# A graph layer's loop on one core: the transposed tile moves to another PSUM bank and TensorE's step is put in another order

## The reference

```
h     = relu(layernorm(x))
p1    = tanh(h @ pp_W1 + pp_b1) @ pp_W2 + pp_b2
inter = concat(p1[src], p1[dst]) @ pi_W1 + pi_b1     # per edge
inter = (inter @ pi_W2 + pi_b2) @ pi_W3              # 64 x 8 values
i1    = einsum('ecb,eb->ec', inter.reshape(E, 64, 8), edge_attr_8)
i1    = tanh(i1 @ ii_W1 + ii_b1) @ ii_W2 + ii_b2
out   = x + segment_sum(i1, dst, 6250)
```

## Time and profile before

| | |
|---|---|
| median of the runs | 2601.27 us |
| the profiled execution | 2618.32 us |
| its span | 2616.5 us |
| PE, DVE, ACT, POOL busy | 71%, 53%, 41%, 58% |
| mean granted clock of PE | 0.81 |

### The profile page before, as it was taken

The page is one execution under the profiler, slowest core; times in us unless marked ns, Lnnn a source line. Parts: engine busy times, 40 slices in busy tenths (PEclk is TensorE's granted clock), DMA queues, the critical chain, the costliest instruction groups (busy, mean ns, idle before and its releaser), DMA issues.

```text
span 2616.5 us, 52109 instructions
## 1 busy us (share of the span) xinstructions
PE 1864.1 (71%) x18378; PEld 1177.1 (45%) x18378; DVE 1383.5 (53%) x2286; ACT 1070.9 (41%) x2409; POOL 1521.1 (58%) x1581
## 2 busy tenths in 40 slices
PE   4277777677777767767677767777777767777777
PEld 3144444444444444444444444444444444444445
DVE  5354555555555545545555555455455554555555
ACT  4144444344444444444444444444444433444444
POOL 2666566566566665565666566666556655566660
PEclk8578878888778788788887887887777877887878
DMA  3322222222222222222222122222222122222221
GB/s 104 68 49 46 47 49 43 47 49 45 48 43 48 48 46 48 46 44 48 48 45 49 43 48 48 46 48 49 44 46 50 43 48 41 48 45 43 45 44 38
DMA packets 311278, 125.86 MB, mean 48 GB/s; under 512 B 233399, under 2 KB 283433, under 8 KB 311161
## 3 DMA queue, kind: packets, MB, share of 16 engines
q1 hardware_dynamic: 259985, 73.19, 14.1%
q0 software_dynamic: 50048, 51.35, 10.4%
q10 hardware_dynamic: 1128, 0.26, 0.1%
HBM read 118.67 MB, written 6.00 MB: 48 GB/s over the span
## 4 chain that ended last, share of the span: by engine, by line
PE 59%; issue 16%; another core or an unknown queue 14%; ACT 7%; DVE 2%; SPq 1%; ACTq 0%; DVEq 0%; DMA 0%
PE bank L1041 34%; PE bank L1048 6%; PE bank L1085 6%; PE spread_ps L1033 4%; PE bank L1025 4%; ACT st_sb L538 4%; PE bank L1017 3%; ACT tt_sb L526 2%; DVE o_sb L697 1%; SPq L277 0%; ACT t_sb L529 0%; PE spread_ps L1125 0%; PE bank L921 0%; DMA v_tab<-acc_all 0%
## 5 line engine op out<-in xcount | busy, mean ns | idle before, releaser
L392 POOL DMA_INDIRECT u_rows<-u_tab,src_e x1564 | 1514.7, 968 | 1034.8 <-PE bank L1025 476.8
L1041 PE MATMUL bank<-o_sb,g_sb 128*64 128x256 f32 x6256 | 1025.7, 484 | 284.8 <-issue 232.2
L697 DVE TENSOR_TENSOR o_sb<-st_sb,spread_ps 128x2048 f32<-128x2048 f32 x391 | 891.3, 2280 | 234.5 <-PE spread_ps L1033 134.0
L1041 PEld LDWEIGHTS bank<-o_sb,g_sb 128*64 128x64 f32 x6256 | 569.8, 171 | 580.0 <-issue 458.5
L538 ACT ACTIVATE st_sb<-bank,s_bias 64x256 f32<-64x256 f32 x1564 | 734.1, 469 | 117.6 <-PE bank L1025 83.2
L795 DVE TENSOR_TENSOR acc_all<-acc_all,bank 65x42 f32 x391 | 76.1, 195 | 919.0 <-remote 640.3
L526 ACT ACTIVATE tt_sb<-bank,z_bias 128x256 f32<-128x256 f32 x391 | 185.5, 474 | 753.0 <-PE bank L1041 386.6
L1048 PE MATMUL bank<-ident,tt_sb 128*128 128x128 f32 x782 | 188.2, 326 | 366.7 <-ACT tt_sb L526 234.4
L529 ACT COPY t_sb<-bank 128x256 f32<-128x256 f32 x391 | 146.5, 375 | 618.8 <-remote 340.8
L1085 PEld LDWEIGHTS bank<-hot,t_sb 128*65 128x65 f32 x3128 | 247.5, 156 | 210.4 <-issue 209.5
L1085 PE MATMUL bank<-hot,t_sb 128*65 128x42 f32 x3128 | 298.0, 251 | 10.8 <-issue 10.2
(11 more groups left out here) (109 smaller groups left out, 227.7 us busy)
## 6 DMA issues: line engine op xcount, KB each, us to landing
loc_bc<-loc_tab SPq DMA_DIRECT2D x391, 126.0 KB
u_rows<-u_tab,src_e POOLq DMA_INDIRECT x1564
v_win<-v_tab SPq DMA_DIRECT2D x391, 15.8 KB
basis<-edge_attr SPq DMA_DIRECT2D x24, 256.0 KB
v_tab<-acc_all SPq DMA_DIRECT2D x6, 375.0 KB
u_tab<-basis SPq DMA_DIRECT2D x6, 250.0 KB
out<-x_sb SPq DMA_DIRECT2D x2, 750.0 KB
x_sb<-x SPq DMA_DIRECT2D x3, 375.0 KB
```

The lines of the kernel that those rows point to most:

```text
L392: pool.indirect_dma_start(out=u_rows[:, g % UR, j, :], out_offset=None, in_=u_tab[:, :], in_offset=bass.IndirectOffsetOnAxis(ap=src_e[:, g ...
L697: return nc.vector.tensor_tensor(o_sb[:, r, :, :].rearrange("p c (j e) -> p j c e", j=TILES), st_sb[:, r, :].rearrange("p (j e) -> p j e", ...
L1041: last = nc.tensor.matmul(z_ps[h * D:(h + 1) * D, 0:2 * P], g_sb[:, c, :], o_sb[:, r, c, 2 * h * P:(2 * h + 2) * P], start=(c == 0), stop= ...
```

## The change

t gets two buffers, the free halves of the banks in which s lies (4 and 5), and leaves z's bank. PE's step n is now: s of n, t of n-3, segment sums of n-4, spread of n-1, z of n-2. ACT's step n is: the copy of s of n, the copy of t of n-3, the tanh of n-2. DVE adds the sums of n-5.

With the buffers the waits change. z waits for the tanh of the group before, no longer for the copy of its t. s of n waits for the copy of t of n-4, which leaves the bank that s is written to. t of n-3 waits for the copy of s of n-1, which reads the same bank, and for the copy of t of n-5.

```
-        z_ps, t_ps = bank[6][:, 0:2 * P], bank[6][:, 2 * P:2 * P + TILES * D]
+        z_ps = bank[6][:, 0:2 * P]
+        t_ps = [bank[4][:, 2 * P:4 * P], bank[5][:, 2 * P:4 * P]]
...
+                    if has(n - 3):
+                        g = n - 3
+                        act.wait_ge(t_ps_ready, g + 1)
+                        if g >= 2:
+                            act.wait_ge(seg_ready, g - 1)
+                        copy_t(g % 2).then_inc(t_ready, 1)
                     if has(n - 2):
...
                         tanh_z(g % 2).then_inc(tt_ready, 1)
-                        act.wait_ge(t_ps_ready, g + 1)
-                        if g >= 2:
-                            act.wait_ge(seg_ready, g - 1)
-                        copy_t(g % 2).then_inc(t_ready, 1)
...
-                    if has(n - 4):
-                        g = n - 4
+                    if has(n - 5):
+                        g = n - 5
...
                 if of(0):
                     if of(2):
                         pe.wait_ge(st_ready, seen(2))
+                    if of(4):
+                        pe.wait_ge(t_ready, seen(4))
...
+                if of(3):
+                    pe.wait_ge(tt_ready, seen(3))
+                    if of(1):
+                        pe.wait_ge(st_ready, seen(1))
+                    if of(5):
+                        pe.wait_ge(t_ready, seen(5))
+                    t_transposes((u - 3) % 2).then_inc(t_ps_ready, 1)
+                if of(4):
+                    pe.wait_ge(t_ready, seen(4))
+                    pe.wait_ge(hot_ready, seen(4))
+                    if of(5):
+                        pe.wait_ge(acc_done, seen(5))
+                    for j in range(TILES):
...
                 if of(2):
                     pe.wait_ge(o_ready, seen(2))
                     if of(3):
-                        pe.wait_ge(t_ready, seen(3))
+                        pe.wait_ge(tt_ready, seen(3))
                     z_group(u % 2).then_inc(z_ready, 1)
-                if of(3):
...
-                if of(2):
-                    pe.wait_ge(tt_ready, seen(2))
-                    t_transposes(u % 2).then_inc(t_ps_ready, 1)
```

More of the change, by code:

```diff
@@ L529, in copy_t @@
                 return nc.scalar.copy(t_sb[:, r, :, 0:D].rearrange("p (h q) c -> p q h c", h=2),
-                                      t_ps.rearrange("p (q h c) -> p q h c", q=2, h=2))
+                                      t_ps[r].rearrange("p (q h c) -> p q h c", q=2, h=2))
             def copy_st(r):
@@ L785, in _ @@
                 for n in STEPS:
-                    if n == 4:
+                    if n == 5:
                         dve.wait_ge(acc_zero, 1)
-                    if has(n - 4):
-                        g = n - 4
+                    if has(n - 5):
+                        g = n - 5
                         start = dve.value_load(base_row[0:1, g:g + 1], min_val=0, max_val=N - W)
@@ L1047, in t_transposes @@
                 for q in range(2):
-                    last = nc.tensor.transpose(t_ps[:, q * P:(q + 1) * P], tt_sb[:, r, q * P:(q + 1) * P], ident[:])
+                    last = nc.tensor.transpose(t_ps[r][:, q * P:(q + 1) * P], tt_sb[:, r, q * P:(q + 1) * P], ident[:])
                 return last
@@ L1067, in step @@
                     add_v(u).then_inc(s_ready, 1)
+                if of(3):
[11 more added lines that the diff above has]
+                    for j in range(TILES):
+                        last = nc.tensor.matmul(seg_ps, t_sb[:, (u - 4) % 2, j, :], hot[:, (u - 4) % HR, j, :],
+                                                start=(j == 0), stop=(j == TILES - 1))
+                    last.then_inc(seg_ready, 1)
                 if of(1):
@@ L1076, in step @@
                     if of(3):
-                        pe.wait_ge(t_ready, seen(3))
+                        pe.wait_ge(tt_ready, seen(3))
                     z_group(u % 2).then_inc(z_ready, 1)
-                if of(3):
-                    pe.wait_ge(t_ready, seen(3))
-                    pe.wait_ge(hot_ready, seen(3))
-                    if of(4):
-                        pe.wait_ge(acc_done, seen(4))
-                    for j in range(TILES):
-                        last = nc.tensor.matmul(seg_ps, t_sb[:, (u - 3) % 2, j, :], hot[:, (u - 3) % HR, j, :],
-                                                start=(j == 0), stop=(j == TILES - 1))
-                    last.then_inc(seg_ready, 1)
-                if of(2):
-                    pe.wait_ge(tt_ready, seen(2))
-                    t_transposes(u % 2).then_inc(t_ps_ready, 1)
             with pe.If(is_fast):
```

## The result

The changed kernel takes 2717.85 us in the median of 4 runs (2711.39 to 2729.8), the kernel before 2603.14 us beside it (2601.23 to 2613.06). The ratio is 1.0438, 95% interval 1.039 to 1.0485: 4.4% slower, where 5% faster was forecast. On another chip of the same type it was 2721.54 against 2609.4 us, 1.0443 [1.0418, 1.0468].

The account below looks back on a forecast made before the run. Bound: a loop of waits, with PE's results seen late while POOL gathers. Gathers 4.8 plus wait 1.2 gave 6.0 us a group, 157 us less; with 5 us for the ends and 24 for loads, about 2470 us, range 2300 to 2660.

Parts of the forecast that it names:

- The loop of the gathers: POOL and PE: s seen, four gathers, then a wait for the next s; 6.41 us a group, forecast 6.0.
- the sum: Loop from s to s: gathers 4.8 plus a wait of 1.2, so 6.0 us a group, 157 us less.
- their wake: POOL's wait for s behind the four gathers: from a mean of 1.62 to about 1.2 us a group.
- s first: PE's s at the step's front: computed about 3.0 us after the last was seen, always well before the gathers end.
- DVE: DVE's sums one step later, product given a whole step, spread seen with s: nothing or a small gain.
- The tanh wait: PE's t waits for tanh, but s is already past it; POOL's 3.35 us waits from there go.
- z's wait for the copy: PE's z no longer waits 0.52 us a group for t's copy; costed at nothing, hidden by the gathers.
- The 24 us for loads: POOL meets a batch of loads about 24 times; 1 us each left for what isn't hidden.
- The double run: Rival: s seen early, POOL runs eight gathers, PE's other results caught behind them; 2838 us if everywhere, chance 0.12.
- The clock: Rival: PE's stand behind z keeps it at 1.2 GHz, 6.5 us a group, about 2640 us; chance 0.07.
- The first rival: s seen during the gathers, so POOL doesn't stop: 5.1 us a group, 2101 us, about 2275 if every second; chance 0.16.

Follow-up runs that it names:

- e4: The kernel before with one of the four gathers of a group, u's other rows left zero: 1658.2 us, one run.
- e6: The kernel before with POOL's gathers replaced by four plain loads a group, issued by SP from fixed places: 1802.67 us, one run.
- e1: The changed kernel with spread moved right behind s (s, spread, t, sums, z): 2568.38 against 2613.09 us for the kernel before, ratio 0.9836.
- e13: The changed kernel with VectorE's addition of the sums four groups back again, not five: 2651.15 against 2609.4 us for the kernel before, ratio 1.0164.
- e3: The changed kernel with the sums moved last (s, t, spread, z, sums): 2576.2 against 2586.72 us for the kernel before, ratio 0.996.
- e7: The changed kernel's order with t left in bank 6, z waiting for t's copy: 2721.87 against 2586.72 us for the kernel before, ratio 1.0502.
- e2: The kernel before, order unchanged, with t in banks 4 and 5 and the waits this brings: 2653.7 against 2613.09 us, ratio 1.0169.
- e9: The changed kernel with VectorE's addition four groups back again, on another kind of chip: 2060.37 against 2063.63 us for the kernel before, ratio 0.9986.

## Why the prediction was wrong

**The loop of the gathers: right, and not enough.** POOL's line accounts for the whole loss between the profiled executions as it accounted for the time before, and e4 and e6 show that the gathers make it. But the sum took their wake as 1.2 us, once s went first. It is 1.87 in the changed kernel and 1.44 in the best order, e1: (902.9 - 354.1) / 381.25, from the row below, 104 to 2500 us. No order came near 1.2, and the term itself was too small: in all eleven traces on these chips with four gathers POOL waits 1.28 to 1.47 us on average even where s starts before the last gather ends. That alone makes 6.2 us a group of the forecast's 6.0. It doesn't make a slower kernel.

```profile
L393 POOL DMA_INDIRECT u_rows<-u_tab,src_e x1525 | 1493.9, 980 | 902.9 <-issue 354.1 <-remote 274.9 <-PE bank L1028 273.8
```

**s first: the wait covered, the conclusion wrong.** PE's line of s (L1020) has 2.8 us of idle in all, so the new wait for the copy of t costs nothing, as I said. But "s is ready well before they end, always" is false. In 151 of 344 groups PE only starts s after the last gather's end, where it was 133 of 346 before. s went early in its step; what was late was the step. s follows z in PE's order, and I asked only what s waits for, not when the z ahead of it can end.

**DVE: this is the step that failed.** "The product gets a whole step, since spread is seen with s and z comes last in the next step. ... Nothing, or a small gain." Spread isn't seen with s. In PE's new order t and the sums stand between them, and each waits. I put this at nothing; the product's idle time went from 223.3 to 1186.2 us. The sums wait for an addition that VectorE has behind the product of the step before. They did so in the old kernel too, but there they stood behind spread and z (s, spread, z, sums, t), and PE never stood for it. Now product, addition, sums, spread, product is one chain, and z hangs on it ahead of the next s. That "the sums come one step later" I read as a shift, and didn't ask what they had been put in front of. e13 shows the part of the sums' wait: 1.044 to 1.016 on one chip. e3 shows that of the sums' place as a whole. On its chip the new order alone (e7) has 1.050, and with the sums last (e3) it is 0.996; the changed kernel itself wasn't run there.

What spread right behind s is worth is seen in e1's timeline. Product, copy of s and gathers start together, and z is computed while the gathers run:

```profile
1508.71 0.94 POOL L393 DMA_INDIRECT u_rows<-u_tab,src_e  x1 [1.58 <-PE bank L1028]
1508.73 2.29 DVE L700 TENSOR_TENSOR o_sb<-st_sb,spread_ps 128x2048 f32<-128x2048 f32 x1 [3.22 <-PE spread_ps L1036]
1508.79 1.90 ACT L539 ACTIVATE st_sb<-bank,s_bias 64x256 f32<-64x256 f32 x4
...
1509.76 1.95 PE L1044 MATMUL bank<-o_sb,g_sb 128*64 128x256 f32 x16
...
1511.64 0.44 PE L1020 MATMUL bank<-ident,u_rows 128*128 128x128 f32 x2
...
1512.46 0.95 POOL L393 DMA_INDIRECT u_rows<-u_tab,src_e  x1 [0.30 <-issue]
```

The product waits 3.22 us there in a kernel that is faster than both. In the changed kernel it waits 3.44 and 3.31, and there the next s hangs on it. A product's idle time tells nothing until one sees what stands behind its end. In e1 the next s starts at 1511.64, before the last gather has ended (1512.46 + 0.95); so it does in 304 of 364 groups.

**The tanh wait: half right.** PE stands for it 445.4 us. It doesn't hold the s of its own step, as I said. With spread and z behind it, it holds the next one's. e3 says that alone costs nothing (0.996). The table of the two waits says it is dear where the sums' wait falls in the same step: 3.18 us against 1.82. So the DVE step and this one failed together. On the chips where the changed kernel is slower, no run has the sums ahead of spread with t behind it.

**z's wait for the copy: costed at nothing.** In the new order, with the banks' change against without, the loss is 4.4% against 5.0%, on different chips. In the old order its removal, with the banks' waits, costs 1.7% (e2).

**The 24 us for loads.** No row shows this term. In the earlier trace rows POOL has no wait for a load. Behind the earlier trace rows stands VectorE's preparation (L757, 3.05 us from 1510.58), which comes ahead of the product.

**The rivals.** None had this mechanism. The double run (0.12) gives a slower kernel in another way and was priced at 2838. The changed kernel isn't that: it has 5 such runs where the kernel before has 12. It has more waits of 2 to 4 us instead. The clock didn't fall: 0.81 against 0.82. The first rival, gathers one behind the other, came true on two chips for the variants profiled there. But by its time (2064 and 2067 us, against the 2101 written down) so it did for the kernel before, so that is the chip and not the change. The changed kernel itself wasn't run on them.

## What to carry to other kernels

When a step of an engine's program is written in a new order, write down for each item what it waits for and what stands ahead of *that* on its own engine, and follow the row round until it closes. Here the row was product, addition, sums, spread, product, and putting the sums ahead of spread closed it. What releases the longest instruction of the row (spread, for the product) goes ahead of whatever waits for that instruction's end. Two waits that cost little each (1.82 and 1.71 us of POOL's waiting, against 1.46 with neither) can cost much in one step (3.18). An idle time counts by what hangs on its end, not by its size.

## What the runs showed of the hardware

**PE's answers and POOL's gathers.** On the chips where the kernel before takes about 2600 us, many answers of PE reach ACT and VectorE about 1.1 us after the last gather, and POOL 1.3 to 1.5 us after it. With four gathers a group the kernel before takes 2587 to 2613 us, with one 1658, with plain loads of the same size 1803. The Trainium skill (TensorE: Matmul & The Clock Gate, "The cost: per-tile semaphore tail") gives the tail of matmuls that share the array as tiles: 25 ns plus 4.7 a tile and 26.3 an increment. For one tile and one increment that would be 56 ns, as an estimate from that page, and s isn't a matmul of that kind. In the timeline of the changed kernel it is over a microsecond: s is computed by 1523.74 and the gather ends at 1524.22, but POOL starts at 1525.64. The rule that the prediction takes from the Trainium skill (SBUF — State Buffer, "SBUF: two separate sides"), that the two kinds of ports can't contend, may hold for the ports. The delay shown here is between a matmul's end and the start of the engine that waited for it, and no run shows where it arises.

**Chips differ in it.** On two of the chips the kernel before takes 2063.63 and 2066.69 us, where on the others it takes 2587 to 2613. This is e9 on the first of the two. POOL's line for the whole run, and then the copy of an s:

```profile
L393 POOL DMA_INDIRECT u_rows<-u_tab,src_e x1564 | 1497.6, 958 | 519.5 <-issue 470.5 <-DMA u_tab<-basis 43.2 <-PE bank L1028 5.8
```

```profile
1508.01 0.94 POOL L393 DMA_INDIRECT u_rows<-u_tab,src_e  x1 [0.30 <-issue]
1508.22 0.42 PE L1028 MATMUL bank<-hot_t,v_win 126*64 126x256 bf16 x2
...
1508.69 1.92 ACT L539 ACTIVATE st_sb<-bank,s_bias 64x256 f32<-64x256 f32 x4 [0.50 <-PE bank L1028]
```

The single gather shown takes the same there, 0.94 us. But ACT has the answer 0.05 us after s is done (1508.64), in the middle of a gather. POOL hardly waits for PE, 5.8 us in all: 470.5 us of issue gaps are 0.30 each. A group is 4 x (0.958 + 0.30) = 5.03 us, and 391 of them are 1967 of the 2060 us. The mean granted clock is 0.89, where it was 0.81. There the gathers are the bound, and the five orders tried lie between 0.996 and 1.006. No profile shows why the chips differ. A ratio from one chip says little about another one: the order of e1 was worth 1.6% where PE's answers are late, and it wasn't run where they aren't.
